# Layer 0 of a four-layer decoder: values computed for two head groups at once, without transposes

## The chip, the cores and the metric

The kernel runs on one core of a Trainium2 chip. The metric is the device time of one execution in microseconds; the kernel is one launch. The core has five engines with a queue each: TensorE (PE, matrix products; its weight loads are shown apart as PEld), VectorE (DVE), ScalarE (ACT), GpSimd (POOL) and SyncE (SP), which here only issues DMA transfers. Every engine works through its own instructions in order and meets the others at semaphores.

## The reference, cut to what matters

Four layers follow each other on x of 2 x 256 tokens by 512 features. Each adds a gated cross-attention and then a gated feed-forward part. The attention of layer 0 is what the change is about: 32 query heads of 128 in 8 groups of 4, each group sharing one key and one value head, over a context of 2 x 512 tokens.

```python
q = (query @ Wq + bq).reshape(B, L, NKV, G, HDIM)
k_, v_ = jnp.split(kv @ Wkv + bkv, 2, axis=-1)
scores = jnp.einsum('blkgd,bmkd->bkglm', q, k) * scale
attn = jax.nn.softmax(scores, axis=-1)
o = jnp.einsum('bkglm,bmkd->blkgd', attn, v).reshape(B, L, NHEAD * HDIM)
return o @ Wo + bo
...
x = x + jnp.tanh(g_xattn[0]) * _L0_xattn_ref(_layernorm(x, axis=-1), ctx_4096, ...)
```

Layer 1 has the same form with a rotary embedding, a causal mask and 256 keys. Its feed-forward weights are stored as 4-bit codes: a weight is a table value `NF4[code]` times a block's scale. The rows of the softmax sum to one.

## The kernel before, in words

**Numbers.** Each product is made of three: an operand is kept as a rounded part (`_hi`) and the rest (`_lo`), and `three` (L370) issues hi x hi, lo x hi and hi x lo for each of the four chunks of the 512 features, 12 matmuls in all, into one PSUM bank. So each result that is used again is evicted by ScalarE (hi) and then by VectorE (lo = result - hi). Weights are loaded in fp32 and split in the same way by ScalarE (`w_high`, L618) and POOL (`w_low`, L631).

**Heads and slots.** The attention of a layer is walked through (`walk`, L248) by groups g, four heads h = 0 to 3 in each, and in a head of layer 0 by four slots j = 0 to 3 (two batches by two tiles of 128 queries). Groups are taken two by two in a loop, so a group has a parity (`g.par`); `last` marks the eighth. Every engine has its own `head` function with the same slots in the same order. On TensorE (L862) slot (h, j) is: scores for the slot two ahead (3 matmuls of 512 columns, into psS, which has two buffers); the four transposes of this slot's probabilities (psT, L761); at j = 0 the product with the values for the second batch of the head before, at j = 2 for the first batch of this one (`weighted_v`, L769: 12 matmuls of 256 columns into psO); a query projection two heads ahead where `q_slot` says so (`q_proj`, psQ); and the units of the slot, from `outs` and `prep` (L62 to L67), which go to the two banks of psX (`use`, L787). The engines beside it: VectorE takes the row maximum (`row_max`), ScalarE the exponential with its sum (`row_exp`), VectorE the reciprocal, POOL multiplies (`norm`, L1247), TensorE transposes, ScalarE writes pT_hi (L1127) and VectorE pT_lo (L934), for which `weighted_v` waits.

**Units of layer 0.** "out" t: one of four tiles of the output projection for the group before (12 matmuls; VectorE adds it to x_sb). "k" 0 and 1: the next group's keys for one batch. "v" 0 and 1: its values for one batch, computed as features by tokens, with the value weights as the stationary operand and 512 context columns moving; VectorE adds the bias and copies them to `scr`. "t" 0 and 1: four transposes of `scr` to tokens by features, which ScalarE and VectorE evict into v_hi and v_lo. Outputs stand at (0,1), (0,2), (0,3), (1,0); the other units at (1,3) k0, (2,0) k1, (2,3) v0, (3,1) t0 and v1, (3,3) t1. The first group has no output tiles, and before it `prologue` (L843) makes k0 k1 v0 v1 t0 t1; the last has no k, v and t, and `tail` makes its four output tiles as "end". Layer 3 (kind "rms") makes its values in another way already: "n" units with the context tile stationary and the weights moving, 24 matmuls of 256 columns.

**Table lookup.** Beside layer 0's attention, one 32nd of layer 1's coded weights is looked up in each head: ScalarE writes four straight lines through the table's lower points at j = 0 and four through the upper ones at j = 2 (`dq_scalar`, L445 to L458), VectorE takes minima at j = 1 and maxima at j = 3 (`dq_vector`), POOL adds the two and multiplies with the scales at the end of j = 3 (`dq_gpsimd`, L481), and SP stores the result. ScalarE's lines at j = 0 wait for the product of the head before (`dq_done`).

**Loads.** SP issues in each head the query weights for three heads on, at h = 0 the next group's key and value weights (one transfer, `load_wkv`, L667) and the group's output weights (`load_wo`), and then the lookup's transfers (`dq_sync`, L424). Splits are put into slots by `SPLIT_TILES` (L60).

Of the kernel before, what the change touches and what calls it, by code (L numbers as in the profile page):

```python
# [21 lines left out]
F32 = mybir.dt.float32  # L22
# [6 lines left out]
P = 128  # L29
B = 2  # L30
SQ = 256
# [26 lines left out]
OUT_SPREAD = {(0, 2): [0], (0, 3): [1], (1, 0): [2], (1, 2): [3]}  # L58
# [24 lines left out]
COUNTERS = ("wqA_dma wqB_dma wkv_dma wo_dma vec_dma wq_hi wq_lo wkv_hi wkv_lo wo_hi wo_lo "  # L83
# [46 lines left out]
class Layer:  # L130


    def __init__(self, index, sems):
        cfg = ATTN[index]
        self.i, self.kind, self.hd, self.n = index, cfg["kind"], cfg["hd"], cfg["groups"]
        self.keys, self.nbuf, self.ahead, self.prep = cfg["keys"], cfg["nbuf"], cfg["ahead"], cfg["prep"]
        self.kt, self.q_slot, self.settle = self.keys // P, cfg["q_slot"], cfg["settle"]
        self.slots, self.outs, self.splits = cfg["slots"], cfg["outs"], cfg["splits"]
# [6 lines left out]
        self.flat = [u for slot in self.prep.values() for u in slot]  # L145
        every = [u for h in range(G4) for j in range(self.slots) for u in self.plan(h, j)]
        prepared = set(self.flat)
        self.order = {u: i for i, u in enumerate(every)}
        self.last_order = {u: i for i, u in enumerate(
            [u for u in every if u not in prepared and u != ("q", G4 - 1)])}  # L150
        self.first_order = {u: i for i, u in enumerate([u for u in every if u[0] != "out"])}
        order = dict(bias="k0 k1 v0 v1 t0 t1", plain="k0 k1 k2 v0 v1 t0 v2 t1 t2").get(self.kind)
# [7 lines left out]
        self.total_x = len(self.first) - 4 + len(self.order) * (n - 1) + len(self.last_order) + 4  # L160
        self.act_letters = "t" if self.rope else "nk" if self.rms else "kt"
        act_uses = len([u for u in self.flat if u[0] in self.act_letters])
        s = self.group_slots * n
        total = dict(wqA_dma=32 * n, wqB_dma=32 * n, wkv_dma=16 * n, wo_dma=16 * n, vec_dma=self.n_vec,
                     wq_hi=4 * n, wq_lo=4 * n, wkv_hi=2 * n, wkv_lo=2 * n, wo_hi=4 * n, wo_lo=4 * n,
# [8 lines left out]
        (wqA_dma, wqB_dma, self.wkv_dma, self.wo_dma, self.vec_dma, self.wq_hi, self.wq_lo, self.wkv_hi,  # L174
         self.wkv_lo, self.wo_hi, self.wo_lo, self.q_mm, self.q_hi, self.q_lo, self.q_f, self.q_sum,
# [7 lines left out]
    def use(self, g, what):  # L183
# [10 lines left out]
        order = self.last_order if g.last else self.order  # L194
        c = len(self.first) - 4 + order[what]
        return g.at(len(self.order), c), (c + len(self.order) * g.par) % 2

    def plan(self, h, j):

        out = [("out", t) for t in self.outs.get((h, j), [])]  # L200
        if self.rms and j == 0:
            out.append(("q", h))
        return out + self.prep.get((h, j), [])

    def slot_uses(self, g, h, j):

        order = self.last_order if g.last else self.order
        first = g.loop is None and g.off == 0
        return [u for u in self.plan(h, j) if u in order and not (first and u[0] == "out")]
# [5 lines left out]
    def count(self, g, letters, what):  # L215


        mine = [u for u in self.flat if u[0] in letters]
        at = mine.index(what) + 1
        return at if g is None else g.at(len(mine), len(mine) + at)  # L220
# [1703 lines left out]
```

## Time and profile before

| | |
|---|---|
| median of 3 runs | 2109.14 us (2109.1 to 2109.63) |
| profiled execution | 2109.25 us, span 2107.5 us |
| TensorE busy | 1955.3 us, 93% of the span |
| VectorE | 1396.2 us, 66% |
| ScalarE | 1049.7 us, 50% |
| GpSimd | 939.8 us, 45% |
| mean granted TensorE clock | 0.966 |

The span runs from the first to the last instruction of the profiled execution. Busy times of different engines lie beside each other, so they don't add up. A matmul's time in the trace reaches from its start to the modelled end of its results; matmuls overlap, and what one costs in a stream is the distance from its start to the next start. Layer 0 takes about the first quarter of the span.

### The profile page before, as it was taken

Reading aid. Unit: us, or ns where it says so; the run is one execution under the profiler, and the core shown is the slowest. Engines: PE = TensorE matmul, PEld = TensorE weight load, DVE = VectorE, ACT = ScalarE, POOL = GpSimd, SP = SyncE. Lnnn points to the kernel's source line nnn. Section 1 sums busy time; section 2 is a strip of 40 time slices with the busy share of each in tenths; the row PEclk is TensorE's granted clock in tenths of the full one; section 3 lists DMA queues with packets and bytes.
Section 4 is the critical chain, followed back from the end, with each engine's and each line's share of the span. In section 5 each row is a group of like instructions: output and inputs, shape, how many; then the busy total and the mean of one; then the engine's idle time right before and its main releaser. Section 6 shows DMA issues by size and latency. Waiting matters only on the chain.

```text
span 2107.5 us, 33700 instructions
## 1 busy us (share of the span) xinstructions
PE 1955.3 (93%) x11106; PEld 1659.7 (79%) x11106; DVE 1396.2 (66%) x2507; ACT 1049.7 (50%) x2405; POOL 939.8 (45%) x1006
## 2 busy tenths in 40 slices
PE   6999999999778999998998999998799999999998
PEld 4788888888557888887667888887678888888886
DVE  5777777777668888888234555556466766676665
ACT  3766676666425444453123544543155555555552
POOL 2655455554546665664322332324144444444432
PEclk9999999999879999999988999999899999999999
DMA  3212322122301211111220101001101110111001
GB/s 143 76 47 76 90 75 75 45 82 65 100 32 36 78 51 55 65 35 65 63 60 5 35 8 35 23 1 56 55 16 45 48 47 26 37 46 46 24 13 46
DMA packets 47072, 106.82 MB, mean 51 GB/s; under 512 B 6064, under 2 KB 21936, under 8 KB 43104
## 3 DMA queue, kind: packets, MB, share of 16 engines
q1 hardware_dynamic: 46944, 105.14, 15.8%
q8 instruction: 77, 1.26, 0.2%
q14 instruction: 51, 0.42, 0.1%
HBM read 98.37 MB, written 6.75 MB: 50 GB/s over the span
## 4 chain that ended last, share of the span: by engine, by line
PE 71%; DVE 13%; issue 6%; ACT 6%; POOL 3%; DMA 0%; DVEq 0%; ACTq 0%; POOLq 0%; SPq 0%
PE psX L375 26%; PE psS L375 12%; PE psQ L375 12%; PE psO L375 11%; PE psT L766 6%; DVE pT_lo L936 2%; PE psT L375 1%; ACT pT_hi L1131 1%; PE psX L839 1%; ACT dq_space L457 1%; DVE p_sb L920 1%; POOL qscr L484 1%; POOL qscr L487 1%; ACT p_sb L1124 1%; POOL p_sb L1256 1%
## 5 line engine op out<-in xcount | busy, mean ns | idle before, releaser
L1256 POOL TENSOR_SCALAR p_sb<-p_sb,rrec 128x512 f32<-128x512 f32 (+1 forms) x320 | 263.6, 824 | 698.5 <-DVE rrec L932 698.5
L1131 ACT ACTIVATE pT_hi<-psT 128x512 fp32r<-128x512 f32 (+2 forms) x384 | 235.0, 612 | 301.8 <-PE psT L766 301.6
L936 DVE TENSOR_TENSOR pT_lo<-psT,pT_hi 128x512 fp32r<-128x512 f32 (+2 forms) x384 | 271.2, 706 | 114.2 <-ACT pT_hi L1131 113.6
L375 PE MATMUL psO<-pT_hi,v_hi 128*128 128x256 f32 (+1 forms) x832 | 256.0, 308 | 40.3 <-DVE pT_lo L936 27.1
L766 PE MATMUL psT<-ident,p_sb 128*128 128x128 f32 x1600 | 243.3, 277 | 13.8 <-POOL p_sb L1256 10.2
L766 PEld LDWEIGHTS psT<-ident,p_sb 128*128 128x128 f32 x1600 | 196.2, 142 | 52.9 <-POOL p_sb L1256 15.4
L375 PE MATMUL psO<-pT_lo,v_hi 128*128 128x256 f32 (+1 forms) x832 | 237.8, 286 | 0.0
L375 PE MATMUL psO<-pT_hi,v_lo 128*128 128x256 f32 (+1 forms) x832 | 237.6, 286 | 0.0
L375 PE MATMUL psQ<-xnT_hi,wq_hi 128*128 128x512 f32 (+1 forms) x448 | 189.5, 423 | 8.6 <-DVE qscr L898 5.7
L375 PEld LDWEIGHTS psO<-pT_hi,v_hi 128*128 128x128 f32 (+1 forms) x832 | 155.7, 187 | 52.4 <-DVE pT_lo L936 40.0
L1124 ACT ACTIVATE p_sb<-psS,nbias 128x512 f32<-128x512 f32 (+1 forms) x192 | 145.2, 756 | 90.9 <-DVE nbias L926 90.9
L375 PE MATMUL psS<-kT_hi,q_hi 128*128 128x512 f32 (+2 forms) x448 | 170.3, 380 | 21.2 <-ACT p_sb L1124 16.1
L375 PE MATMUL psQ<-xnT_lo,wq_hi 128*128 128x512 f32 (+1 forms) x448 | 180.9, 404 | 0.0
L375 PE MATMUL psQ<-xnT_hi,wq_lo 128*128 128x512 f32 (+1 forms) x448 | 180.6, 403 | 0.0
L375 PE MATMUL psX<-wo_hi,oT_hi 128*128 128x512 f32 (+1 forms) x432 | 173.4, 401 | 1.6 <-DVE oT_lo L960 1.6
L635 POOL TENSOR_TENSOR wq_lo<-wq_f,wq_hi 128x512 fp32r<-128x512 f32 (+1 forms) x112 | 141.3, 1263 | 64.8 <-ACT wq_hi L623 64.8
L375 PE MATMUL psX<-wo_hi,oT_lo 128*128 128x512 f32 (+1 forms) x432 | 169.3, 392 | 0.0
L375 PE MATMUL psX<-wo_lo,oT_hi 128*128 128x512 f32 (+1 forms) x432 | 169.1, 391 | 0.0
L375 PE MATMUL psS<-kT_hi,q_lo 128*128 128x512 f32 (+2 forms) x448 | 163.5, 365 | 0.0
L375 PE MATMUL psS<-kT_lo,q_hi 128*128 128x512 f32 (+2 forms) x448 | 163.4, 365 | 0.0
L926 DVE TENSOR_REDUCE nbias<-psS 128x1 f32<-128x512 f32 (+1 forms) x192 | 147.8, 770 | 22.8 <-PE psS L375 22.8
L1124 ACT ACTIVATE p_sb<-p_sb,nbias 128x512 f32<-128x512 f32 x128 | 92.7, 724 | 140.5 <-DVE nbias L924 140.4
(366 smaller groups left out, 4914.5 us busy)
## 6 DMA issues: line engine op xcount, KB each, us to landing
wq_f<-in_a_wq SPq DMA_DIRECT2D x96, 256.0 KB, 2.7
wo_f<-in_a_wo SPq DMA_DIRECT2D x24, 1024.0 KB, 5.0
wkv_f<-in_a_wkv SPq DMA_DIRECT2D x24, 512.0 KB, 3.8
mask_sb<-in_codes SPq DMA_DIRECT2D x32, 174.0 KB, 2.4
qscr<-in_amax SPq DMA_DIRECT2D x32, 174.0 KB, 2.3
w<-qscr SPq DMA_DIRECT2D x32, 174.0 KB, 1.9
wo_f<-in_f_wT SPq DMA_DIRECT2D x3, 1024.0 KB, 5.3
wq_f<-in_a_wq SPq DMA_DIRECT2D x16, 192.0 KB, 2.3
```

Of the source, the lines that this page charges most:

```text
L375: mm = pe.matmul(dst, w, m, start=(first and k == 0), stop=(last and k == n - 1))
L457: ins = act.activation(tiles[q], dq_codes[h % 2], ACT.Copy, scale=slope, bias=NF4[c] - slope * c)
L484: pool.tensor_tensor(chord_above[0], chord_below[0], chord_above[0], ALU.add).then_inc(dq_sum, 1)
L487: pool.tensor_tensor(dq_w, chord_above[0], dq_w, ALU.mult).then_inc(dq_done, 1)
L635: L.wq_lo.inc(pool.tensor_tensor(lo, f, hi.bitcast(F32), ALU.subtract))
L766: mm = pe.transpose(t_view(L, j)[:, i, :], p_view(L, j, h)[:, m * P:(m + 1) * P], ident[:, :])
L839: mm = pe.matmul(X[:, m:m + 1], qscr[:, h % 2, m * P:(m + 1) * P], ones[:, 0:1], start=True, stop=True)
L926: L.s_max.inc(dve.tensor_reduce(nbias[:, j:j + 1], s_view(L, j), AX.X, ALU.max, negate=True))
L936: L.t_lo.inc(dve.tensor_tensor(pT_view(L, pT_lo, j), t_view(L, j), pT_view(L, pT_hi, j).bitcast(F32), ALU.subtract))
L1124: L.s_exp.inc(act.activation(p_view(L, j), src, ACT.Exp, bias=nbias[:, j:j + 1], accum_out=rsum[:, j:j + 1]))
L1131: L.t_hi.inc(act.activation(pT_view(L, pT_hi, j), t_view(L, j), ACT.Copy))
L1256: L.s_norm.inc(pool.tensor_scalar(p_view(L, j), p_view(L, j), rrec[:, j:j + 1], 1.0, ALU.mult, ALU.mult))
```

## The change: what it does

- Layer 0's "v" and "t" units are replaced by "n" units: 128 context tokens are the stationary operand, and the value weights of two neighbouring groups (2 x 128 columns) move. Unit n(i) makes the values of tiles 2i and 2i + 1 for both groups, tokens by features at once: 24 matmuls of 256 columns. n0 and n1 are made at (3,2) and (3,3) of the odd group before, n2 and n3 at (0,0) and (0,1) of the even group. The prologue makes k0 k1 n0 n1.
- The value bias is no longer added to the values but to the head's result: `o_high` and `o_low` add it to psO.
- Value weights are loaded apart from key weights, two transfers per two groups at h = 2 of the even group, into half of `wkv_f` and `scr`; they are split at (0,3) and (1,1) of the odd group. Output weights are split one head later: (2,1), (2,3), (3,1), (3,3).
- Outputs stand at (0,3), (1,0), (1,2), (1,3). Keys stand at (2,1) and (3,1) in even groups and at (2,2) and (2,3) in odd ones; `q_slot` is (2, 1, 3, 3) in even and (1, 1, 1, 1) in odd groups. The first head's oT of an odd group gets a place of its own (`place`).
- The lookup's lines are written two in each slot: lower 0 and 3 at j = 0, upper 0 and 1 at j = 1, upper 2 and 3 at j = 2, lower 1 and 2 of the next head at j = 3 (behind waits for `dq_low` and the next codes).
- Layer 1: its transposes "t0" move from (3,1) to (3,0). Its two-slot heads, its units and its schedule are otherwise as before.

```diff
+OUT_SPREAD = {(0, 3): [0], (1, 0): [1], (1, 2): [2], (1, 3): [3]}
+SPLIT_ROWS = dict(wq=[(h, 2) for h in range(4)], wkv=[(0, 1)], wv=[(0, 3), (1, 1)],
+                  wo=[(2, 1), (2, 3), (3, 1), (3, 3)])
 SPLIT_TILES = dict(wq=[(h, 2) for h in range(4)], wkv=[(0, 1), (0, 3)], wo=[(1, 1), (1, 3), (2, 1), (2, 3)])
 SPLIT_PAIRS = dict(wq=[(h, 0) for h in range(4)], wkv=[(0, 0), (0, 1)], wo=[(2, 0), (2, 1), (3, 0), (3, 1)])
 ATTN = [
-    dict(kind="bias", hd=128, groups=8, keys=512, slots=4, nbuf=2, ahead=2, settle=2, q_slot=(1, 1, 1, 3),
-         outs=OUT_EARLY, splits=SPLIT_TILES,
-         prep={(1, 3): ["k0"], (2, 0): ["k1"], (2, 3): ["v0"], (3, 1): ["t0", "v1"], (3, 3): ["t1"]}),
+    dict(kind="bias", hd=128, groups=8, keys=512, slots=4, nbuf=2, ahead=2, settle=2,
+         q_slot=((2, 1, 3, 3), (1, 1, 1, 1)), outs=(OUT_SPREAD, OUT_SPREAD), splits=SPLIT_ROWS,
+         prep=({(0, 0): ["n2"], (0, 1): ["n3"], (2, 1): ["k0"], (3, 1): ["k1"]},
+               {(2, 2): ["k0"], (2, 3): ["k1"], (3, 2): ["n0"], (3, 3): ["n1"]})),
     dict(kind="rope", hd=128, groups=8, keys=256, slots=2, nbuf=2, ahead=2, settle=2, q_slot=(0, 0, 1, 1),
          outs=OUT_PAIRS, splits=SPLIT_PAIRS,
-         prep={(2, 0): ["k0"], (2, 1): ["v0"], (3, 1): ["t0"]}),
+         prep={(2, 0): ["k0"], (2, 1): ["v0"], (3, 0): ["t0"]}),
...
+        def dq_lines(act, tiles, side, codes, which):
+            for q in which:
+                c = side + 2 * q
+                slope = NF4[c + 1] - NF4[c]
+                ins = act.activation(tiles[q], codes, ACT.Copy, scale=slope, bias=NF4[c] - slope * c)
+            return ins
+
         def dq_scalar(act, g, h, j):
-            if j not in (0, 2):
-                return
-            first = g.loop is None and g.off == 0 and h == 0
+            codes = dq_codes[h % 2]
             if j == 0:
+                first = g.loop is None and g.off == 0 and h == 0
                 act.wait_ge(dq_code[h % 2], g.at(32, 16 * (h // 2 + 1)))
                 if not first:
                     act.wait_ge(dq_done, g.at(4, h))
-            side, tiles, ready = (0, chord_below, dq_below) if j == 0 else (8, chord_above, dq_above)
-            for q in range(4):
-                c = side + 2 * q
-                slope = NF4[c + 1] - NF4[c]
-                ins = act.activation(tiles[q], dq_codes[h % 2], ACT.Copy, scale=slope, bias=NF4[c] - slope * c)
-            ins.then_inc(ready, 1)
+                dq_lines(act, chord_below, 0, codes, range(4) if first else (0, 3)).then_inc(dq_below, 1)
+            elif j == 1:
+                dq_lines(act, chord_above, 8, codes, (0, 1))
+            elif j == 2:
+                dq_lines(act, chord_above, 8, codes, (2, 3)).then_inc(dq_above, 1)
+            elif not (g.last and h == G4 - 1):
+                act.wait_ge(dq_low, g.at(4, h + 1))
+                act.wait_ge(dq_code[(h + 1) % 2], g.at(32, 16 * ((h + 1) // 2 + 1)))
+                dq_lines(act, chord_below, 0, dq_codes[(h + 1) % 2], (1, 2))
...
+            if L.two and (h, j) in L.splits["wv"] and g.par and not g.last:
+                out.append(("wv", g.to(1), L.splits["wv"].index((h, j))))
...
+            if kind == "wv" and piece == 0:
+                return [z[:, 1, :] for z in (wkv_f, wkv_hi, wkv_lo)]
+            if kind == "wv":
+                return [scr[:, 0, :]] + [z[:, 0, 4 * SQ:6 * SQ] for z in (pT_hi, pT_lo)]
...
+        def wv_chunk(c):
+            at = (c % 2) * 2 * P
+            return [z[:, at:at + 2 * P] for z in w_parts(layers[0], "wv", c // 2)[1:]]
...
+            def load_wv(g):
+                L.wv_lo.wait(sp, g.half(2, 0))
+                for piece in (0, 1):
+                    L.wv_dma.inc(sp.dma_start(w_parts(L, "wv", piece)[0], names["wv"][g.half(1, 0), :, piece, :]), 16)
...
+                load_wv(Group(0))
                 dq_sync(sp, None, 0)
...
+                if L.two and h == 2 and g.par == 0 and not (g.loop is None and g.off == L.n - 2):
+                    load_wv(g.to(2))
...
                 elif kind == "n":
-                    L.wkv_lo.wait(pe, gp.at(2, 2))
+                    if L.rms:
+                        L.wkv_lo.wait(pe, gp.at(2, 2))
+                    elif i == 0:
+                        L.wv_lo.wait(pe, 2 if g is None else g.half(2, 4))
                     for z in (0, 1):
                         at = (2 * i + z) * P
                         mm = three(pe, X[:, z * 2 * P:(z + 1) * 2 * P],
-                                   [([m[:, c, at:at + P] for m in (cT_hi, cT_lo)], [w[:, c, :] for w in wkv_rows])
-                                    for c in range(DC)])
+                                   [([m[:, c, at:at + P] for m in (cT_hi, cT_lo)],
+                                     [w[:, c, :] for w in wkv_rows] if L.rms else wv_chunk(c)) for c in range(DC)])
...
+        def v_pair(v, i):
+            return v[:, :, 2 * i * P:2 * (i + 1) * P].rearrange("p z (t d) -> p z t d", d=P)
+
+        def x_pair(X):
+            return X.rearrange("p (t z d) -> p z t d", z=2, d=P)
...
+                lo, hi = oT_view(L, 1, g, h), oT_view(L, 0, g, h).bitcast(F32)
+                if L.two:
+                    bv = vecs[:, bass.ds(g.at(1, 5 * L.n), 1)]
+                    L.o_lo.inc(dve.scalar_tensor_tensor(lo, psO[:, :], bv, hi, ALU.add, ALU.subtract))
+                else:
+                    L.o_lo.inc(dve.tensor_tensor(lo, psO[0:hd, :], hi, ALU.subtract))
...
+                elif kind == "n" and L.two:
+                    ins = dve.tensor_tensor(v_pair(v_lo, i), x_pair(X), v_pair(v_hi, i).bitcast(F32), ALU.subtract)
...
-                elif kind == "v" and L.kind == "bias":
-                    bv = vecs[:, bass.ds(gp.at(1, 5 * L.n), 1)]
-                    ins = dve.tensor_scalar(scr[:, i % 2, :], X, bv, None, ALU.add)
...
-                L.o_hi.inc(act.activation(oT_view(L, 0, g, h), psO[0:hd, :], ACT.Copy))
+                if L.two:
+                    act.sem_inc(wait_met, 1)
+                    bv = vecs[:, bass.ds(g.at(1, 5 * L.n), 1)]
+                    L.o_hi.inc(act.activation(oT_view(L, 0, g, h), psO[:, :], ACT.Identity, bias=bv))
+                else:
+                    L.o_hi.inc(act.activation(oT_view(L, 0, g, h), psO[0:hd, :], ACT.Copy))
...
+                    L.x_act.inc(act.activation(v_pair(v_hi, i), x_pair(X), ACT.Copy))
```

## Rows read from the trace of the kernel before

**Rows 1.** The page, part 1: busy time (share of the span) and instructions.

```profile
PE 1955.3 (93%) x11106; PEld 1659.7 (79%) x11106; DVE 1396.2 (66%) x2507; ACT 1049.7 (50%) x2405; POOL 939.8 (45%) x1006
```

**Rows 2.** Busy us by stretch: PE, PEld, DVE, ACT, POOL, clock; groups 0, 3, 7.

```profile
46.00:111.40 65.40, 61.00 (x338) 50.95 (x338) 47.26 (x93) 47.14 (x112) 37.88 (x37) 0.97 0.21 64
...
242.30:307.68 65.38, 64.16 (x360) 54.56 (x361) 47.88 (x91) 44.29 (x103) 35.59 (x34) 1.00 0.25 73
...
503.89:575.05 71.16, 58.85 (x296) 49.23 (x296) 46.86 (x88) 37.74 (x87) 33.49 (x32) 0.88 0.28 87
```

**Rows 3.** Waits of TensorE, 111.4 to 503.9 us: total, times, longest.

```profile
PE psO L375 <- DVE pT_lo L936: 6.1, 12, 0.6
PE psX L375 <- DVE oT_lo L960: 1.6, 7, 0.3
```

**Rows 4.** TensorE in order of time: start us, us, instruction [idle before].

```profile
329.59 0.60 PE L766 MATMUL psT<-ident,p_sb 128*128 128x128 f32 x4
329.94 0.36 PE L375 MATMUL psO<-pT_hi,v_hi 128*128 128x256 f32 x1
...
331.45 0.40 PE L375 MATMUL psS<-kT_hi,q_hi 128*128 128x512 f32 x1
...
332.15 0.60 PE L766 MATMUL psT<-ident,p_sb 128*128 128x128 f32 x4
...
335.36 0.39 PE L375 MATMUL psS<-kT_hi,q_hi 128*128 128x512 f32 x1
...
358.52 0.60 PE L766 MATMUL psT<-ident,p_sb 128*128 128x128 f32 x4
359.66 0.38 PE L375 MATMUL psO<-pT_hi,v_hi 128*128 128x256 f32 x1 [0.54 <-DVE pT_lo L936]
```

**Rows 5.** The other engines in order of time ahead of that wait.

```profile
353.12 1.54 POOL L641 TENSOR_TENSOR wo_lo<-wo_f,wo_hi 128x512 fp32r<-128x512 f32 x1
...
356.67 1.65 ACT L457 ACTIVATE dq_space<-mask_sb 128x348 f32<-128x348 int32 x4 [0.59 <-POOL qscr L487]
...
358.83 0.69 DVE L936 TENSOR_TENSOR pT_lo<-psT,pT_hi 128x512 fp32r<-128x512 f32 x1 [1.43 <-ACT pT_hi L1131]
```

**Rows 6.** Groups by line, layer 0 and its steady groups: busy us, mean ns.

```profile
L833 PE MATMUL psX<-ident,scr 128*128 128x128 f32 x56 | 8.4, 272 | 0.0
...
L1001 DVE TENSOR_SCALAR scr<-psX,vecs 128x512 f32<-128x512 f32 x12 | 8.8, 737 | 0.0
```

**Rows 7.** TensorE in order of time in layer 3, an n unit's ends.

```profile
1644.65 0.36 PE L375 MATMUL psX<-wkv_hi,cT_hi 128*128 128x256 f32 x1
...
1647.60 0.40 PE L375 MATMUL psS<-kT_hi,q_hi 128*128 128x512 f32 x1
```

**Rows 8.** The prologue: VectorE in order of time, then the chain.

```profile
23.66 1.22 DVE L402 TENSOR_TENSOR cT_lo<-qscr,cT_hi 128x1024 fp32r<-128x1024 f32 x1
...
33.37 5.80 PE psX L375 x24
```

**Rows 9.** Waits of TensorE in group 0, 43 to 111.4 us.

```profile
PE psO L375 <- DVE pT_lo L936: 2.9, 4, 1.5
```

**Rows 10.** Group 7: waits of TensorE from 503.9 us; busy by stretch.

```profile
PE psO L375 <- DVE pT_lo L936: 5.6, 4, 1.6
PE psT L766 <- POOL p_sb L1256: 4.1, 2, 2.8
...
536.00:540.00 4.00, 1.20 (x6) 0.96 (x7) 1.86 (x5) 3.44 (x9) 1.39 (x3) 0.81 0.42 117
540.00:544.00 4.00, 4.00 (x18) 3.60 (x17) 2.87 (x6) 2.48 (x7) 3.07 (x3) 0.50 0.05 19
```

**Rows 11.** The chain of waits behind layer 0's attention.

```profile
564.75 4.65 DMA wq_f<-in_a_wq
```

**Rows 12.** Waits of TensorE in layer 1, 660 to 980 us.

```profile
PE psO L375 <- DVE oT_lo L960: 13.2, 9, 1.8
```

More of the change, by code:

```diff
@@ L135, in __init__ @@
         self.i, self.kind, self.hd, self.n = index, cfg["kind"], cfg["hd"], cfg["groups"]
-        self.keys, self.nbuf, self.ahead, self.prep = cfg["keys"], cfg["nbuf"], cfg["ahead"], cfg["prep"]
-        self.kt, self.q_slot, self.settle = self.keys // P, cfg["q_slot"], cfg["settle"]
-        self.slots, self.outs, self.splits = cfg["slots"], cfg["outs"], cfg["splits"]
+        self.keys, self.nbuf, self.ahead = cfg["keys"], cfg["nbuf"], cfg["ahead"]
+        self.kt, self.settle = self.keys // P, cfg["settle"]
+        self.slots, self.splits = cfg["slots"], cfg["splits"]
+        self.two = cfg["kind"] == "bias"
+        self.q_slots, self.outs, self.preps = (
+            cfg[z] if self.two else (cfg[z], cfg[z]) for z in ("q_slot", "outs", "prep"))
+        self.spare_place = cfg["outs"] is not OUT_EARLY
         self.pairs = self.slots == 2
@@ L144, in __init__ @@
         self.masked = self.rms or self.rope
-        self.flat = [u for slot in self.prep.values() for u in slot]
-        every = [u for h in range(G4) for j in range(self.slots) for u in self.plan(h, j)]
+        self.flats = [[u for slot in prep.values() for u in slot] for prep in self.preps]
+        self.flat = self.flats[1]
+        every = [[u for h in range(G4) for j in range(self.slots) for u in self.plan(par, h, j)] for par in (0, 1)]
         prepared = set(self.flat)
-        self.order = {u: i for i, u in enumerate(every)}
+        self.orders = [{u: i for i, u in enumerate(e)} for e in every]
+        self.n_x = len(every[0])
+        assert self.n_x == len(every[1]) and self.n % 2 == 0
         self.last_order = {u: i for i, u in enumerate(
-            [u for u in every if u not in prepared and u != ("q", G4 - 1)])}
-        self.first_order = {u: i for i, u in enumerate([u for u in every if u[0] != "out"])}
-        order = dict(bias="k0 k1 v0 v1 t0 t1", plain="k0 k1 k2 v0 v1 t0 v2 t1 t2").get(self.kind)
+            [u for u in every[1] if u not in prepared and u != ("q", G4 - 1)])}
+        self.first_order = {u: i for i, u in enumerate([u for u in every[0] if u[0] != "out"])}
+        order = dict(plain="k0 k1 k2 v0 v1 t0 v2 t1 t2").get(self.kind)
         self.first = order.split() if order else self.flat + ([("q", -1)] if self.rms else [])
@@ L243, in place @@
     def place(self, g, h):
-        return G4 if h == 0 and g.par and self.outs is not OUT_EARLY else h
+        return G4 if h == 0 and g.par and self.spare_place else h
 def walk(eng, L, prologue, head, tail):
@@ L626, in w_high @@
                 L.wkv_hi.inc(act.activation(hi, f, ACT.Copy))
+            elif kind == "wv":
+                L.wv_dma.wait(act, g.half(32, 32))
+                L.wv_hi.inc(act.activation(hi, f, ACT.Copy))
             else:
@@ L772, in weighted_v @@
                     L.o_lo.wait(pe, g.at(4, h) if g.off or g.loop is not None or h else 0)
-                    if h == 0:
+                    if h == 0 and not (L.two and g.par):
                         prev = g.to(-1) if g.off else None
                         L.x_free.wait(pe, L.use(prev, L.flat[-1])[0] + 1)
+                elif h == 0 and L.two and not g.par:
+                    L.x_free.wait(pe, L.use(g, "n3")[0] + 1)
                 pairs = []
@@ L874, in head @@
                         weighted_v(g, h, 0)
-                    if j == L.q_slot[h] and L.head(g, h, L.q_lead):
+                    if j == L.q_slot(g, h) and L.head(g, h, L.q_lead):
                         q_proj(*L.head(g, h, L.q_lead))
@@ L1160, in use @@
                     k_hi = k_cols(gp.par, i * CTX, CTX)[0]
-                if kind == "n":
+                if kind == "n" and L.two:
+                    L.x_mm.wait(act, k + 1)
+                    L.x_act.inc(act.activation(v_pair(v_hi, i), x_pair(X), ACT.Copy))
+                elif kind == "n":
                     L.x_mm.wait(act, k + 1)
@@ L1216, in head @@
                         row_exp(*nxt)
-                    if j == L.q_slot[h] and L.head(g, h, L.q_lead) and not L.rope:
+                    if j == L.q_slot(g, h) and L.head(g, h, L.q_lead) and not L.rope:
                         q_high(*L.head(g, h, L.q_lead))
@@ L1263, in use @@
             def use(g, what):
-                if what[0] not in "knq" or what[0] == "out":
+                if what[0] not in "knq" or what[0] == "out" or L.two:
                     return
@@ L1303, in head @@
                         norm(*L.step(g, h, j, L.settle))
-                    if j == L.q_slot[h] and L.rope and L.head(g, h, L.q_lead):
+                    if j == L.q_slot(g, h) and L.rope and L.head(g, h, L.q_lead):
                         q_sum(*L.head(g, h, L.q_lead))
```

71 lines of the change are left out of this document (40 added, 31 removed).

## The prediction

> **What bounds the kernel now.** I read the page's first part, then the busy time by stretch, then what TensorE waited for, then TensorE in order of time beside the other engines. TensorE is busy 1955.3 of 2107.5 us, the next engine 1396.2 [rows 1]. The change touches layer 0 (about 0 to 575 us) and one entry of layer 1. Six of layer 0's eight head groups repeat in 65.4 us, 61.0 to 64.2 of it TensorE busy at granted clock 1.00 or nearly; VectorE has 48 and ScalarE 44 [rows 2]. So in the steady groups TensorE sets the time, and a microsecond counts if it is TensorE's work or one of its stalls.
>
> The stalls: over the six groups 12 waits of weighted_v for pT_lo (6.1 us idle) and 7 of an output tile for oT_lo (1.6 us) [rows 3], so two and one per group. What one costs is seen start to start. Undisturbed, weighted_v starts 0.35 us after the probability transposes (329.59, 329.94), the disturbed one 1.14 us after (358.52, 359.66) [rows 4]: 0.79 us each, 0.53 of it shown as idle and 0.26 refilling. The output tile's wait shows 0.23; with some refill I count 0.37. Together 1.95 us a group.
>
> What ends that wait: after POOL's wo_lo (353.12) and the lookup's sum and product, ScalarE may write the four lower lines of the next lookup, 1.65 us at 356.67, and only behind them comes pT_hi, so pT_lo starts at 358.83 and ends at 359.52 [rows 5]. That is layer 0's limiting chain: lookup product, four lines, pT_hi, pT_lo, weighted_v.
>
> **The change, part by part.**
>
> *Value transposes go.* 16 "t" units of four transposes in layer 0. TensorE starts four in 0.35 us [rows 4]: 16 x 0.35 = 5.6 us less, 0.7 a group. The row of these transposes gives 272 ns for one [rows 6], but that is latency which overlaps. The Trainium skill (TensorE: Matmul & The Clock Gate, "Part 4: PE-mode transpose") gives about 275 ns for one in a kernel's context; the duration agrees, the spacing in this trace does not, and by the page's figure 64 transposes would be worth 17.6 us.
>
> *Values side by side.* A "v" unit was 12 matmuls of 512 columns: from 332.15 + 0.35 to 335.36, 2.86 us [rows 4]. An "n" unit is 24 of 256 columns with the context tile as weights; the fourth layer has just this form: 1644.65 to 1647.60, 2.95 us [rows 7]. 16 units by 0.09, or 1.5 us more; bounds 0 (the smallest difference, where refill is alike) and 3.2 us (0.2 a unit). The same page ("Back-to-back issue gap") gives N / 2.4 + 2.5 ns per matmul, so 12 more matmuls would cost 0.03 us a unit; the row's 0.09 is used.
>
> *Evictions.* v's copy on VectorE (737 ns, row of L1001 [rows 6]) goes, 16 times; t's ACT and DVE pair is replaced one for one by n's. The value bias moves to o_high and o_low (32 each); a VectorE pass with a bias took 737 ns, one without 690 [rows 5, 6], so about 0.05 us more on each engine. They hide: the output tile that reads oT comes two slots later. If that cover failed it would be 0.1 us a head, 3 us. Only the last, before the four end tiles, is exposed: 0.1 us, left out.
>
> *Order of the slots.* Before, (2,3) to (3,3) and (0,0) to (0,1) were crowded on ScalarE and VectorE (t0 with v1, t1 with a q) and some odd slots had no unit. After, every odd slot of a steady group holds one 2.86 us unit, and the second half of the four slots holds weighted_v (1.51 us, 329.94 to 331.45 [rows 4]). Out 0 at (0,3) has a slot and a half after oT_lo: that wait goes, and I see nothing late in its place.
>
> *Lookup two by two.* ScalarE writes two lines in each slot instead of four in two. Between the product and pT_hi stand two lines: 0.83 us less against a lateness of 0.79 [rows 4, 5]. But slot (3,1) no longer holds t0, so weighted_v falls due up to 0.4 us earlier: 0 to 0.4 us of that wait can stay. The second wait (four upper lines ahead of pT_hi at (3,3)) loses the same 0.83 and the value evictions too. The new waits at j = 3 (dq_low, the next codes) were met two slots before; queued behind them are only the next pT_hi.
>
> The weak place is the light head: odd slots one unit, even slots only weighted_v, 12.8 us (4 x 1.05, 2 x 1.51, 2 x 2.86). Even groups have two (heads 2, 3), odd ones one (head 0), twelve in all. VectorE's share of a head is (48 - 2 x 0.74) / 4, or 11.6 us less about 0.4 for the output tiles it hasn't: 11.2, 88%. It fits, but each reciprocal and o_low also waits on ScalarE, and POOL's wo_lo still stands before the lookup's sum at (2,3) and (3,3). I put 0.35 us a group for stalls kept or new (bounds 0 and 2.0).
>
> Per steady group: -0.7 + 0.2 - 1.95 + 0.35 = -2.1; six make -12.6.
>
> *Weights and DMA.* The bytes are the same; SP issues two wv transfers per two groups at head 2, split eleven slots later. In the prologue they wait for the last cT_lo (23.66 + 1.22 = 24.9 [rows 8]); with the 4.65 us that a weight transfer took elsewhere on the chain [rows 11] they are there by 29.6, and ScalarE's first pass and POOL's two (1.54 us each, as wo_lo [rows 5]) need 3.7 more: 33.3. The third psX unit starts at 33.37 now [rows 8]: just hidden, I take 0; without cover, up to 3 us once. ScalarE is held meanwhile, with q_high and k0's kT_hi queued behind it, which that unit waits for: within the same bound.
>
> *Group 0.* The prologue has two value units less, moved into slots (0,0) and (0,1), which have idle time now: TensorE idles 2.9 us for pT_lo early in this group [rows 9]. But k0 leaves (1,3), which becomes bare. I take -3 us with the shorter prologue; bounds 0 and -6.
>
> *Group 7.* It takes 71.2 us instead of 65.4 [rows 2]: without the next group's units heads 2 and 3 have only 1.05 and 2.6 us slots, and TensorE idles 5.6 us for pT_lo and 4.1 for POOL's norm [rows 10]. Outs 2 and 3 fall into (1,2) and (1,3), that was bare, and the lookup's chain, on which the bare heads run, is 0.83 us shorter in each of two heads: -3.5 us, bounds 0 and -7. It is passed on: the next layer's first weight transfer, at 564.75 on the chain, is issued behind this lookup's last store [rows 11], so the stage behind starts as much earlier. The wo_lo added at (3,3) falls into POOL's idle time.
>
> *Layer 1, t0 from (3,1) to (3,0).* Slot (3,0) has no unit, and at (3,1) weighted_v waits for oT_lo, 13.2 us in nine waits [rows 12]. t0's 0.35 us moves into that wait, in seven groups: -2.4. VectorE gets v_lo earlier, which could push the row maximum; I take -2.2, bounds +2 and -3.
>
> **Sum.** -12.6 - 3 - 3.5 - 2.2 = -21.3 us. The profiled execution took 2109.25 us (span 2107.5 and 1.75 around it), the median is 2109.14: 2088.
>
> **Rivals.**
> 1. *The stalls only move.* Each light head gives back what the crowded slots gave: at 12.8 us against a VectorE of 11.2 plus its waits a stall of 0.8 to 1 us a head is enough. Then the six groups keep 0.5 each, and ends and layer 1 some 5: 2101. For it: VectorE at 88%, POOL's wo_lo unchanged. Against: in group 0's later heads and the steady ones VectorE idles 17 of 65 us, and mostly for others.
> 2. *More than that.* All stalls go and both ends give their full bound: -14.7 - 6 - 7 - 2.4, or 2079.
> 3. *A transpose occupies TensorE for its 272 ns.* Then 64 are 17.4 us, not 5.6: 2076. The page above would have it so. Against: four start in 0.35 us with work right behind them.
> 4. *Nothing.* A wait for wv or the norm in each group eats the gain, 2107.
> 5. *Slower: light heads let the clock drop.* At 536 to 540 us TensorE was busy 1.20 of 4.00 us, and behind it the granted clock is 0.50 [rows 10]: the lower of the two levels, 1.2 GHz. A light head run so costs some 10 us more (12.8 x 0.8). If lookup and VectorE starve TensorE in the light heads as in group 7's bare ones, it is slower from three of the twelve: 2088 + 3 x 10 + 1, or 2119. Against: a light head has 12.8 us of work, a bare one 7.2.
>
> **Chances.** Forecast 0.55 (own range 2083 to 2094), stalls move 0.22, more 0.10, transposes 0.03, nothing 0.05, slower 0.05. About 0.2% (4.2 us) can be told from no change in this kernel. Faster by more: 0.55 + 0.22 + 0.10 + 0.03, less 0.02 for the upper edge of "stalls move", 0.88; within: 0.07; slower: 0.05. The range 2079 to 2103 leaves out the last two cases and the edges.
>
> **What would show it.** A steady group of 62.9 to 63.7 us (two of them 126.6) with TensorE's busy time down by about 0.9 only. No wait of psX for oT_lo at out 0; at (3,2) and (0,2) waits of pT_lo below 0.4 us, each lookup group on ScalarE of two. n units at 2.95 us. Group 7 under 69 us, layer 1's groups 0.35 us shorter. It is wrong if light heads take over 13.5 us, if the waits for pT_lo in the six groups still sum to over 6 us, or if n units take over 3.1.

## The result, and the profile after

The changed kernel took 2084.65 us (median of four, 2082.53 to 2085.68) against 2109.12: 24.5 us less; the ratio is given as 0.9897, with a 95% interval of 0.987 to 0.9923 (the two medians by themselves give 0.9884). The forecast was 2088.

The page after, part 1, answers to [rows 1]: TensorE 15.6 us less busy, a bare 7 us less on VectorE.

```profile
PE 1939.7 (93%) x11234; PEld 1658.9 (80%) x11234; DVE 1389.3 (67%) x2491; ACT 1052.9 (51%) x2405; POOL 935.3 (45%) x1006
```

Busy times by stretch (length, then PE, PEld, DVE, ACT, POOL, clock), for a pair of groups between its first output tiles and for group 7 with its tail (like the 71.16 us before, from the end of the query projection at (0,1)), answer to [rows 2]:

```profile
110.67:236.54 125.87, 125.78 (x755) 109.97 (x754) 94.50 (x177) 89.34 (x204) 70.64 (x69) 1.00 0.25 77
...
484.31:551.71 67.40, 56.47 (x297) 46.58 (x296) 47.56 (x87) 37.35 (x86) 32.69 (x32) 0.92 0.32 102
```

A steady group is 62.9 us long instead of 65.4, and TensorE is busy throughout, but for 0.09 us in some pairs: the list of its waits over the six groups, two lines before [rows 3], is empty. Busy time fell by 1.3 us a group, the period by 2.5. In a light head, behind the lookup product that [rows 5] show ahead of the old stall, the trace after reads so (TensorE, ScalarE, VectorE and POOL in order of time; head 3 of an even group):

```profile
343.07 0.94 POOL L512 TENSOR_TENSOR qscr<-qscr 128x348 f32<-128x348 f32 x1
...
344.10 0.88 ACT L465 ACTIVATE dq_space<-mask_sb 128x348 f32<-128x348 int32 x2 [0.94 <-POOL qscr L512]
344.89 0.58 ACT L1195 ACTIVATE pT_hi<-psT 128x512 fp32r<-128x512 f32 x1
...
345.50 0.69 DVE L997 TENSOR_TENSOR pT_lo<-psT,pT_hi 128x512 fp32r<-128x512 f32 x1 [0.96 <-ACT pT_hi L1195]
...
346.23 0.60 PE L816 MATMUL psT<-ident,p_sb 128*128 128x128 f32 x4
...
346.58 0.36 PE L391 MATMUL psO<-pT_hi,v_hi 128*128 128x256 f32 x1
```

Same chain, two lines in it instead of four: pT_lo ends at 346.19, 0.39 us before TensorE reaches the product. Two lines more, some 0.8 us, would make it 0.4 late (an estimate). The third light head of the pair, head 0 of the odd group, has no such slack:

```profile
359.07 0.69 DVE L997 TENSOR_TENSOR pT_lo<-psT,pT_hi 128x512 fp32r<-128x512 f32 x1 [0.59 <-ACT pT_hi L1195]
359.13 0.60 PE L816 MATMUL psT<-ident,p_sb 128*128 128x128 f32 x4
359.82 0.38 PE L391 MATMUL psO<-pT_hi,v_hi 128*128 128x256 f32 x1
```

Here the product starts 0.69 us after the transposes instead of 0.35, behind a pT_lo that ends at 359.76. This happens once in each pair, and the list of waits does not show it, because the transposes' modelled ends cover nearly all of it.

The n unit, in this layer (TensorE; the next scores follow at 298.67, as forecast 2.95 us later):

```profile
295.72 0.36 PE L391 MATMUL psX<-wkv_hi,cT_hi 128*128 128x256 f32 x1
```

Where the time came from, by marks in the profiled executions (starts on TensorE, us; "behind" runs from layer 1's first end tile to the start of the last residual addition of an output tile, in layer 3; no kernel of this study differs in its instructions there):

| kernel | pair of steady groups | layer 1's first q projection | its first end tile | behind | median |
|---|---|---|---|---|---|
| before | 130.87 | 614.72 | 978.91 | 1108.6 | 2109.12 |
| after | 125.87 | 591.04 | 955.51 | 1107.7 | 2084.65 |
| after, again | 125.88 | 593.11 | 957.16 | 1109.6 | 2087.0 |
| lookup by two alone | 126.75 | 595.57 | 957.40 | 1102.6 | 2084.79 |
| the same, again | 126.75 | 593.54 | 957.68 | 1105.3 | 2084.3 |
| all but the lookup | 130.43 | 612.50 | 976.72 | 1107.9 | 2106.83 |
| outputs early | 130.05 | 604.57 | 969.22 | 1107.3 | 2097.95 |
| lookup alone, t twice | 128.52 | 601.07 | 963.29 | 1113.3 | 2097.55 |
| t0 of layer 1 back | 125.87 | 592.13 | 956.02 | 1108.4 | 2084.77 |
| output weights split earlier | 126.03 | 590.75 | 955.27 | 1109.8 | 2085.76 |
| o_low first | 125.87 | 591.99 | 956.54 | 1107.7 | 2085.71 |
| end of layer 0, t0 back | 126.06 | 587.28 | 949.03 | 1109.9 | 2079.88 |

Layer 0 and the stage behind it gave 23.7 us, layer 1 gave none. The column "behind" moves by 10.7 us between kernels that have the same instructions there. Most of that arises in one stretch, some 410 to 615 us behind the end tile, and goes with the granted clock. The same 1017 matmuls in the lookup alone and in "lookup alone, t twice" (busy times by stretch, in the order given above):

```profile
1368.70:1566.20 197.50, 167.68 (x1017) 146.57 (x1015) 116.63 (x223) 80.23 (x182) 69.47 (x80) 0.94 0.13 42
```

```profile
1374.70:1579.20 204.50, 175.19 (x1017) 153.69 (x1015) 116.49 (x223) 80.42 (x182) 69.68 (x80) 0.90 0.12 41
```

By these means the clock stood at the lower of its two levels (1.2 GHz) for about 24 of the 197.5 us and for about 41 of the 204.5 us (an estimate from the two rows), and 7.0 of the 10.7 us lie here. What made the clock differ under the same instructions no run shows. So end to end a difference of a few us between two of these kernels says little about an edit; the stage columns say more. The kernel before itself had medians of 2106.94 to 2110.65 in the later sets.

### The profile page after: what moved, and what is told of

Its sections match the earlier page's. It is cut to its first block, busy times and chain, and to the rows that moved or that the text cites. A ratio compares the mean times of both kernels' runs of the same rounds, so it can differ in the third digit from the quotient of the medians.

```text
span 2083.1 us, 33965 instructions
## 1 busy us (share of the span) xinstructions
PE 1939.7 (93%) x11234; PEld 1658.9 (80%) x11234; DVE 1389.3 (67%) x2491; ACT 1052.9 (51%) x2405; POOL 935.3 (45%) x1006
## 3 DMA queue, kind: packets, MB, share of 16 engines
q1 hardware_dynamic: 48096, 105.14, 15.8%
## 4 chain that ended last, share of the span: by engine, by line
PE 75%; DVE 11%; issue 6%; ACT 5%; POOL 2%; DMA 0%; DVEq 0%; SPq 0%; ACTq 0%; POOLq 0%
PE psX L391 27%; PE psS L391 13%; PE psQ L391 12%; PE psO L391 12%; PE psT L816 7%; PE psT L391 1%; PE psX L894 1%; ACT p_sb L1184 1%; DVE p_sb L981 1%; DVE nbias L975 1%; DVE pT_lo L997 1%; DVE p_sb L972 1%; ACT pT_hi L1195 1%; DVE nbias L985 1%; DVE ln_stat L519 1%
## 5 line engine op out<-in xcount | busy, mean ns | idle before, releaser
L391 PE MATMUL psX<-wo_hi,oT_hi 128*128 128x512 f32 (+1 forms) x416 | 166.8, 401 | 4.3 <-DVE oT_lo L1024 4.3
L391 PE MATMUL psX<-wo_hi,oT_lo 128*128 128x512 f32 (+1 forms) x416 | 163.7, 393 | 0.0
L678 POOL TENSOR_TENSOR wo_lo<-wo_f,wo_hi 128x512 fp32r<-128x512 f32 (+1 forms) x112 | 148.0, 1322 | 34.6 <-ACT wo_hi L663 33.3
L391 PE MATMUL psX<-wo_lo,oT_hi 128*128 128x512 f32 (+1 forms) x416 | 163.2, 392 | 0.0
```

Source lines behind the costliest of these rows:

```text
L391: mm = pe.matmul(dst, w, m, start=(first and k == 0), stop=(last and k == n - 1))
L678: L.wo_lo.inc(pool.tensor_tensor(lo, f, hi.bitcast(F32), ALU.subtract))
```

## The experiments

**1. The lookup two by two, alone, in the kernel before.** `dq_scalar` of the changed kernel is put into the kernel before; nothing else.

```diff
-            side, tiles, ready = (0, chord_below, dq_below) if j == 0 else (8, chord_above, dq_above)
-            for q in range(4):
-                ...
+                dq_lines(act, chord_below, 0, codes, range(4) if first else (0, 3)).then_inc(dq_below, 1)
+            elif j == 1:
+                dq_lines(act, chord_above, 8, codes, (0, 1))
+            elif j == 2:
+                dq_lines(act, chord_above, 8, codes, (2, 3)).then_inc(dq_above, 1)
+            elif not (g.last and h == G4 - 1):
+                ...
+                dq_lines(act, chord_below, 0, dq_codes[(h + 1) % 2], (1, 2))
```

> The kernel before, with only the lookup's lines written two by two. Theory A (that chain ended both waits for pT_lo, 0.79 us each in each group): steady groups fall from 65.4 to 63.9 us, the 12 waits for pT_lo (6.1 us) all but vanish, the 7 for oT_lo stay; about 10 us faster than before. Rival B (the crowded slots with v and t units made the waits): they stay at 0.5 us each and the time moves by less than 2 us.

Measured: 2084.79 us, ratio 0.9886 (0.9864 to 0.9909). The steady group fell from 65.4 to 63.4 us, and TensorE's list of waits there is empty, that for oT_lo included:

```profile
297.23:360.61 63.38, 63.38 (x362) 54.59 (x360) 48.02 (x91) 44.43 (x103) 35.40 (x34) 1.00 0.25 76
```

Theory A held and was too small: not 1.5 but 2.0 us a group, since the third wait went too, and 19.1 us by layer 1's first projection. Of these, 12.2 are in the six steady groups and 4.3 ahead of them, in group 0 (its successor's first output tile starts at 107.11 instead of 111.43); the rest is in group 7 and the stage behind it, where "about 10 us" had counted nothing. I had put the third wait down to where the output tiles stood; no output tile was moved here.

**2. Everything but the lookup.** The changed kernel with the old `dq_scalar`, so the diff of experiment 1 the other way:

```diff
-                dq_lines(act, chord_below, 0, codes, range(4) if first else (0, 3)).then_inc(dq_below, 1)
-                ...
+            side, tiles, ready = (0, chord_below, dq_below) if j == 0 else (8, chord_above, dq_above)
+            for q in range(4):
+                ...
```

> The changed kernel with the lookup's lines written as before, four in slots 0 and four in slots 2. Theory A (the limiting chain is lookup product, lines, pT_hi, pT_lo, weighted_v): in the light heads pT_hi comes 0.8 us later, TensorE waits for pT_lo again in three heads per two groups, and a pair of groups takes 127.0 to 129 us instead of 125.9: 4 to 11 us slower in all. Rival B (the even spread of the units alone removed the stalls): no wait for pT_lo in the steady groups, pairs at 125.9 us, the same time.

Measured: 2106.83 us, ratio 0.9998 (0.9982 to 1.0013): no gain at all. First the waits of TensorE from 115.5 to 507 us (sum, times, longest), then one pair of groups with its busy times:

```profile
PE psO L391 <- DVE pT_lo L988: 11.1, 15, 1.2
```

```profile
245.98:376.42 130.44, 126.84 (x756) 110.07 (x754) 93.82 (x177) 89.71 (x204) 71.29 (x69) 1.00 0.24 73
```

Five waits for pT_lo a pair, where the kernel before had four, and up to 1.2 us long instead of 0.6: a light head ends sooner, the lookup chain doesn't. Theory A had expected three. Rival B falls. The new order of slots removed TensorE work and idled it away; it was 22 us slower than with the lookup by two, twice what theory A gave at most.

**3. Both again, on one chip.** The changed kernel and the lookup alone, with no edit to either.

> The changed kernel unaltered, to stand beside the lookup alone on one chip. Theory A (by the profile's stages, the lookup two by two brings layer 0's end 19.2 us forward and the rest of the change 4.5 us more; the equal medians of the first comparison come from parts of the program that no edit touches): 3 to 6 us below the kernel with the lookup alone. Rival B (the rest of the change is worth nothing end to end): within 2 us of it.

> The kernel before with only the lookup's lines two by two, again. Theory A: layer 1's first query projection at 595.5 us in the profile as before, 4.5 us behind the changed kernel's, and the stretch behind layer 1's attention, which took 5.5 us less than in the five other profiles, is back at 1107 to 1109 us: 2088 to 2090 us. Rival B: that stretch stays at 1102 to 1103 us, so that the lookup alone ends level with the changed kernel.

Measured: 2087.0 us (ratio 0.99, 0.9877 to 0.9922) and 2084.3 (0.9888, 0.9866 to 0.991). Theory A's 3 to 6 us did not appear: the changed kernel is 2.7 us above the lookup alone, just outside rival B's 2 as well. By stage: the pair of groups is 0.87 us shorter in the changed kernel both times, but layer 1's first projection starts 4.5 us sooner in one comparison and 0.4 in the other, because the stretch from group 7's first output tile to that projection varies by itself: 102.85 and 105.46 us in the changed kernel, at a mean granted clock of 0.86 and 0.83, and 108.22 and 106.84 us in the lookup alone. The rest of the change is worth 2.6 us in the six groups; that it is worth anything end to end is not shown. The "behind" stretch of the lookup alone was 1105.3, between A's and B's; the two rows under the table show the clock that goes with such a difference.

**4. The output tiles back at their old slots, in the changed kernel.**

```diff
-         ... outs=(OUT_SPREAD, OUT_SPREAD), splits=SPLIT_ROWS,
+         ... outs=(dict(OUT_EARLY), dict(OUT_EARLY)), splits=SPLIT_ROWS,
```

> The changed kernel with the output tiles back at (0,1), (0,2), (0,3), (1,0). Theory A (the wait of out 0 for oT_lo was a late effect of the same lookup chain, gone with two lines, as the kernel with the lookup alone shows): in odd groups no wait for oT_lo, the pair of groups within 0.4 us of 125.9, though the slots of heads 0 and 1 are now uneven and bare ones at (1,2), (1,3) of group 7 cost the end of layer 0 1 to 3 us. Rival B (the later place removed it): 0.2 to 0.4 us of wait for oT_lo returns in every group, 2 to 3 us in all in the steady groups.

Measured: 2097.95 us, ratio 0.9961 (0.9943 to 0.9979). No wait for oT_lo, as A said; but the pair takes 130.05 us, 4.2 more or 12.4 in the six groups, where A allowed 0.4 a pair and B 2 to 3 us in all. The waits of TensorE from 105 to 495 us:

```profile
PE psO L391 <- DVE pT_lo L997: 4.9, 8, 0.7
PE psS L391 <- ACT p_sb L1188: 1.9, 6, 0.3
```

Both theories were wrong on why the place counts: early outputs crowd head 0 and leave (1,2) and (1,3) bare, and there the exponential and pT_lo are late (at 130.34 and 132.84 us, for one). My reading is that with a lookup chain of that length each odd slot needs its 2.86 us unit; no run filled (1,3) with other work to show it.

**5. What a value transpose costs.** The lookup alone, each transpose of a t unit issued twice.

```diff
-                    for m in range(4):
+                    for m in [z for z in range(4) for _ in range(2 if L.i == 0 else 1)]:
                         mm = pe.transpose(...)
```

> The kernel before with the lookup two by two, and every value transpose of layer 0 issued twice (eight in a t unit instead of four, the same result). Theory A (four cost TensorE 0.35 us, and nothing hides them now that the steady groups have no wait): steady groups go from 63.38 to 64.1 us, 5 to 6 us in all. Rival B (a transpose holds TensorE for its 272 ns): 65.5 us a group, 17 us in all. Rival C (there is still slack on TensorE): under 0.2 us a group.

```profile
301.11:365.37 64.26, 64.26 (x370) 55.44 (x368) 47.98 (x90) 44.91 (x102) 35.26 (x34) 1.00 0.24 74
```

64.26 instead of 63.38 us a group: eight transposes cost 0.88 us, 0.11 each. That is theory A with 0.44 for four instead of 0.35, and far from the 2.2 of B. The median rose by 13 us, of which the stages before "behind" show 5.6 to 5.9 (963.29 against 957.40 and 957.68), as theory A said; the rest is in the stretch that no edit touches.

**6. Layer 1's t0 back at (3,1).**

```diff
-         prep={(2, 0): ["k0"], (2, 1): ["v0"], (3, 0): ["t0"]}),
+         prep={(2, 0): ["k0"], (2, 1): ["v0"], (3, 1): ["t0"]}),
```

> The changed kernel with layer 1's t0 back in slot (3,1); nothing else differs. Theory A (t0 in (3,0) only turned one wait into three: for v0's copy, for oT_lo and for the next query's rotation): layer 1's steady groups go from 44.7 back to 44.4 us, the waits of the query projection for qscr (7.0 us in seven) and of t0 for scr (2.7 us in seven) vanish, that of weighted_v for oT_lo rises from 6.1 to about 13 us; layer 1 as a whole within 1.5 us either way, since its first full group was 1.3 us shorter after the change. Rival B (the 44.7 comes from something else that layer 0 leaves behind): the groups stay at 44.7 us and t0's place is worth the 2.2 us that the prediction gave it, so this kernel is 2 us slower than the changed one.

Measured: 2084.77 us, ratio 0.9879 (0.9855 to 0.9903). The waits of TensorE in layer 1, first of the changed kernel, from 636 to 956 us:

```profile
PE psQ L391 <- DVE qscr L959: 7.0, 7, 1.0
PE psO L391 <- DVE oT_lo L1026: 6.1, 9, 0.8
PE psX L888 <- DVE scr L1067: 2.7, 7, 0.5
```

and of this one:

```profile
PE psO L391 <- DVE oT_lo L1026: 13.2, 9, 1.8
```

Theory A: one wait of 13.2 us had become three of 15.8, and the steady groups are 44.4 us again instead of 44.7. The layer as a whole comes out within 0.6 us, because its second group takes 46.0 us in this kernel (as before), and 44.7 in the changed one; in the lookup alone that group took 44.4 us once and 46.0 once, so its long form is not tied to t0. Between groups of the same form, then, t0's new place costs 0.3 us each.

**7. The output weights split earlier,** four pieces in head 2.

```diff
-                  wo=[(2, 1), (2, 3), (3, 1), (3, 3)])
+                  wo=[(2, 0), (2, 1), (2, 2), (2, 3)])
```

> The changed kernel with the output weights split at (2,0), (2,1), (2,2), (2,3) instead of (2,1), (2,3), (3,1), (3,3). Theory A (splitting the last piece at (3,3) of group 7 sends the 1 MB load of the next stage's weights into the same microseconds as layer 1's first weights, which then take 7.0 us instead of 4.65, and holds VectorE 3.65 us ahead of oT_lo): that transfer is back below 5.5 us, the first end tile waits under 1 us for oT_lo instead of 4.3, the next stage starts 1.5 to 3 us earlier, and the time is 2 us lower. Rival B (ScalarE and POOL in head 2, a light head in even groups, cannot take four splits in a row): new waits for pT_lo at 0.3 us or more in the steady groups, and the time is equal or up to 4 us higher.

Measured: 2085.76 us, ratio 0.9881 (0.9859 to 0.9903). The end of layer 0 in the changed kernel, in order of time: the 1 MB load, VectorE's first pass over it, oT_lo behind that; and in a fence of its own, from the chain that ended last, the weight transfer:

```profile
533.48 0.33 SPq L1428 DMA_DIRECT2D wo_f<-in_f_wT  x1
...
536.05 0.92 POOL L512 TENSOR_TENSOR qscr<-qscr 128x348 f32<-128x348 f32 x1
...
538.47 1.23 DVE L1450 TENSOR_SCALAR kT_lo<-wo_f 128x2048 fp32r<-128x2048 f32 x1 [3.65 <-DMA wo_f<-in_f_wT]
...
539.61 0.74 DVE L1024 SCALAR_TENSOR_TENSOR oT_lo<-psO,vecs,oT_hi 128x512 fp32r<-128x512 f32 x1
```

```profile
539.04 7.00 DMA wq_f<-in_a_wq
```

and the same two views with the earlier split:

```profile
534.28 1.22 DVE L1450 TENSOR_SCALAR kT_lo<-wo_f 128x2048 fp32r<-128x2048 f32 x1
535.55 0.75 DVE L1024 SCALAR_TENSOR_TENSOR oT_lo<-psO,vecs,oT_hi 128x512 fp32r<-128x512 f32 x1
...
536.35 2.21 DVE L1463 SCALAR_TENSOR_TENSOR kT_hi<-wo_f,kT_lo 128x2048 fp32r<-128x2048 f32 x1
536.45 2.92 POOL L512 TENSOR_TENSOR qscr<-qscr 128x348 f32<-128x348 f32 x1
```

```profile
540.75 4.99 DMA wq_f<-in_a_wq
```

The mechanism of theory A is there (4.99 instead of 7.00 us, no wait for oT_lo at the first end tile), the gain is not (590.75 is 0.3 and 2.4 us ahead of the changed kernel's two): VectorE's pass over 2048 columns now runs beside POOL's product, which takes 2.92 us instead of 0.92. Steady groups lost 0.16 us a pair; rival B's waits did not come. In one point I had misread the trace for theory A. The 1 MB load itself had landed by 538.47, before the second weight transfer was issued at 539.04. What ran beside that transfer are the four loads of 256 KB issued right behind the 1 MB one: the last left at 535.99 and took 7.0 us to land. With the earlier split it had left at 532.94 and took 5.2. And the late wo_lo cost time once more, on the chain that ended last: beside it VectorE's first maximum of the last lookup took 1.62 us, and 0.51 with the earlier split.

**8. Only oT_lo ahead of the threshold pass.**

```diff
-                if L.i == 0:
-                    f0_threshold(dve)
-                elif L.i == 2:
+                if L.i == 2:
                     f2_router(dve)
                 o_low(g, 3)
+                if L.i == 0:
+                    f0_threshold(dve)
```

> The changed kernel with only that o_low ahead of the threshold, so that it no longer waits for the 1 MB weight load. Theory A (the next stage's normalisation waits for POOL, which splits layer 1's first weights, and not for the end tiles): the wait of 4.3 us for oT_lo goes to under 1 us, the four end tiles start 3 to 4 us earlier, and layer 1's first query projection does not move: 591 to 593 us. Rival B (the end tiles are on the path): it starts 2 us or more earlier.

Measured: 2085.71 us, ratio 0.9881 (0.9862 to 0.9899). The 4.3 us wait for oT_lo went, the last of the four end tiles started 2.7 us earlier (546.18 instead of 548.85), and layer 1's first projection stayed at 591.99, between the changed kernel's two: theory A. In the tiles a new wait of 1.75 us, for x_sb, took part of what was won. The 4.3 us were TensorE's longest wait at the layer's end, and taking them away moved nothing behind it.

**9. The three edits together:** the diffs of 6, 7 and 8, and no other.

> The changed kernel with three edits: output weights split in head 2 as in the earlier run, VectorE's o_low of the last head ahead of the next stage's weight threshold, and layer 1's t0 back at (3,1). Theory A (the end of layer 0 hangs on the last lookup product, SP's queue and layer 1's first weights; with the early split alone the product took 2.9 us instead of 0.9 because VectorE's two passes over 2048 columns ran beside it): the product takes 1.0 to 1.3 us, the second weight transfer about 5 us, and layer 1's first query projection starts at 588 to 589 us instead of 591.0 to 593.1; 2 to 4 us below the changed kernel in all. Rival B (something else of that stage is the limit): 590.5 us or later.

Measured: 2079.88 us (2077.92 to 2083.15), ratio 0.9858 (0.984 to 0.9876), the lowest of the study. The product and the transfer, in order of time and from the chain:

```profile
535.81 0.92 POOL L512 TENSOR_TENSOR qscr<-qscr 128x348 f32<-128x348 f32 x1
```

```profile
538.12 4.63 DMA wq_f<-in_a_wq
```

Both short at once, and layer 1's first projection at 587.28, 3.8 and 5.8 us before the changed kernel's two. Rival B falls. Layer 1 took 361.8 us instead of 364.5 up to its first end tile: 0.3 us less in each steady group, and it lacks the long second group (44.4 us here, 46.0 in experiment 6), which is no merit of the edits. Its interval and the changed kernel's overlap by 0.0006, on different chips; by stage the gain shows in the one profiled execution, and by totals it is likely.

## Why the prediction was right, and where it was not

*The bound and the steady groups.* TensorE's work and stalls set the time, and groups came out at 62.9 us, the lower edge of the 62.9 to 63.7 foretold. The three terms held to about 0.1 us: 1.95 us of stalls and 0.7 of transposes less 0.2 for the n units are 2.45, measured 2.5; the lookup alone gave 2.0, the rest on top of it 0.44. Of the 0.35 us a group set aside for light heads 0.17 was used: 0.34 us once in a pair, at (0,2) of the odd group, while head 3 of the even group had 0.39 us to spare. The margin is as thin as feared: experiments 2 and 4 show what happens when it goes. Three small things were off and changed nothing: the 61.0 us of TensorE busy is group 0's row [rows 2], where each steady group has 64.2; the terms of a light head add up to 12.9 us, not 12.8, and the trace after has 12.9 (339.09 to 351.99); and busy time fell by 1.3 us a group, not 0.9, which is no sign of the time won, as the lookup alone shows (0.8 less busy, 2.0 shorter).

*The attribution was wrong in one term.* I gave the lookup the two waits for pT_lo and the new place of the outputs the one for oT_lo (0.37 us a group, 2.2 in all). Experiment 1 shows all three going with the lookup alone. That ScalarE and VectorE carried its delay on to oT_lo is my reading; no trace was followed for it. And I summed the parts as if each had its own worth. They have not: alone the lookup gives 2.0 us a group, the rest 0.2, both 2.5. TensorE work taken out of a head is worth something only when the chain beside it is short enough. What the title names, values for two groups without transposes, gave 0.44 us a group with its new order of slots; the lookup, one bullet among six, gave the rest.

*Group 0 and the prologue.* -3 forecast. The first slot of group 1 starts its scores at 100.27 us; before, the same ones stood at 103.70: -3.4. wv was indeed just in time: the first n unit waited 0.31 us for it, at 32.24.

*Group 7.* -3.5 forecast; 23.7 less 3.4 and 14.9 leaves 5.4 for it and the stage behind, within its bounds; the group took 67.4 us, under the 69 foretold. But the sentence "The wo_lo added at (3,3) falls into POOL's idle time" was half of the truth. POOL had the time, and what I did not follow is who waits for it on SP, and who runs beside it. The next stage's loads start behind wo_lo, and the four of 256 KB among them so fell beside layer 1's first weights (7.00 us instead of 4.65 [rows 11]); and VectorE's pass beside wo_lo took 1.1 us longer (experiment 7). Experiment 9 shows 3.8 us and more to be had there.

*Layer 1.* -2.2 forecast, +0.3 measured (364.19 us before, 364.47 after, up to the first end tile). The failed step is "t0's 0.35 us moves into that wait": t0 in (3,0) has to wait itself for v0's copy, which VectorE does only then, and VectorE's eviction of t0, now earlier, holds up the rotation for the next query projection by 1.0 us a group. I had named that danger for the row maximum with a bound of +2, and taken the wrong end. The +0.3 even flatters the step: the second group, 46.0 us before and 44.7 after, gave 1.3 us that t0's place does not explain (experiment 6), so t0 cost some 0.3 us a group, about 2 us in seven, where 2.2 were to be won.

*The transposes.* 0.11 us each when added (experiment 5), 0.09 by spacing, not 272 ns: the third rival is out. With it goes the figure of the Trainium skill (TensorE: Matmul & The Clock Gate, "Part 4: PE-mode transpose") read as a cost; as a duration it agrees with the trace. The first rival, stalls that only move, describes in kind what the change would have been without its lookup part, though the 2106.83 us of experiment 2 are 6 above its time. The clock stayed at 1.00 in all steady groups.

So the total was right to 3.4 us, and partly by luck, with two errors of opposite sign: layer 1 (+2.5) against steady groups and group 7 (-4.2); group 0 (-0.4) and the stretch behind (-0.9) are most of the rest.

## What to carry to other kernels

When a stall recurs, follow the chain behind it and cut that first: splitting one block of four passes in two gave 2.0 of the 2.5 us a group that this change brought, while everything else, work taken off TensorE included, gave 0.2 until the chain was cut. Price the parts of a change in the order in which they are bounded, not as a sum. Of a step that moves, follow the queue that waits for it (SP here) as far as the next stage's first load, and leave a visible stall alone if another chain ends later.

## What the runs showed of the hardware that I had not expected

POOL's product of 128x348 took 0.92 us alone and 2.92 us while VectorE ran a pass over 128x2048 in fp32 (2.21 us) beside it; the sum before it 1.78 instead of 0.93. With VectorE's pass moved behind it the product took 0.92 again (experiment 9). It goes the other way too: VectorE's maximum of 128x348 took 1.62 us instead of 0.51 while POOL made wo_lo. Both of these VectorE passes read two tiles from SBUF. That is one of the cases for which the Trainium skill (GPSIMD Engine Reference, "1. Specifications") says that the two engines contend for their common SBUF interfaces. The trace agrees, and shows that one such overlap can triple the time of an instruction on either engine.

And instructions that no edit touched, behind layer 1, took 1102.6 to 1113.3 us in twelve profiled executions of ten different programs. Between the two ends of that range the granted clock differs (mean 0.97 and 0.96 over the stretch, 0.94 and 0.90 where most of the time arises), with the same instructions. So does the time of one and the same kernel: the executions of the lookup alone spread over 8 and 11 us in its two sets, those of the changed kernel over 3 and 2. What sets the clock differently from one execution to the next stays open.
